# Scores and maxima of a two-layer transformer in two 64-row tiles of the TensorE array, with the causal mask of the first block of queries added by TensorE

## The reference, cut to what matters

```
x = x + L0_attn(ln(x)) + L0_ffn(ln(x))     # 32 query heads of 16 dims, 8 key heads; full softmax; GELU, 512 -> 2048 -> 512
x = x + L1_attn(ln(x)) + L1_ffn(ln(x))     # the same heads with rotary embedding, causal mask; SiLU gate, 512 -> 2*512 -> 512

scores = einsum('bqhd,bkhd->bhqk', q, k) * SM_SCALE
scores = where(mask, scores, finfo.min)    # second layer only: key <= query
probs  = softmax(scores)
ctx    = einsum('bhqk,bkhd->bqhd', probs, v)
```

## Time and profile before

| | |
|---|---|
| median of 3 runs | 596.59 us (593.41 to 599.78) |
| the profiled execution | 596.43 us |
| its span in the profile | 594.7 us |
| PE busy | 563.2 us, 95% |
| DVE busy | 456.5 us, 77% |
| ACT busy | 348.0 us, 59% |
| POOL busy | 232.6 us, 39% |

### The profile page before, as it was taken

How to read it: one execution, slowest core, us unless ns; L and a number is a source line. 1 busy time by engine, 2 the same in 40 slices (tenths; PEclk the granted TensorE clock), 3 DMA queues, 4 the chain that set the end, 5 groups by cost and what they waited for, 6 DMA issues and landing times.

```text
span 594.7 us, 10503 instructions
## 1 busy us (share of the span) xinstructions
PE 563.2 (95%) x3216; PEld 435.0 (73%) x3216; DVE 456.5 (77%) x1232; ACT 348.0 (59%) x598; POOL 232.6 (39%) x345
## 2 busy tenths in 40 slices
PE   3979999999999999999999999899899999998997
PEld 3967777777777878777787787667677778766754
DVE  6487987765666687577899678898998989789673
ACT  3667756664564676376677276357645564565451
POOL 6231334713304521313223115264745485364242
PEclk9999999999999999999999999999999999999999
DMA  6993452453223244315433323336443443434101
GB/s 200 130 317 103 120 142 69 113 157 107 79 82 108 80 124 136 90 40 174 126 128 99 113 78 101 90 107 143 134 117 89 104 130 109 125 108 133 29 6 68
DMA packets 30535, 67.02 MB, mean 113 GB/s; under 512 B 4880, under 2 KB 18192, under 8 KB 28560
## 3 DMA queue, kind: packets, MB, share of 16 engines
q1 hardware_dynamic: 21840, 38.04, 24.5%
q0 software_dynamic: 8640, 28.32, 15.9%
HBM read 50.87 MB, written 13.63 MB: 108 GB/s over the span
## 4 chain that ended last, share of the span: by engine, by line
PE 79%; DVE 8%; issue 5%; DMA 3%; POOL 2%; ACT 2%; DVEq 0%; POOLq 0%; ACTq 0%
PE banks L766 53%; PE banks L826 8%; PE banks L874 8%; PE banks L852 7%; DMA q_sb<-max_t 2%; DVE banks L1156 2%; PE banks L786 1%; PE banks L855 1%; POOL probs L708 1%; DVE neg_max L1156 1%; DVE o_tok L1177 1%; DVE x_res L1200 1%; PE banks L835 1%; DVE bn L1054 1%; DVE hid L1221 1%
## 5 line engine op out<-in xcount | busy, mean ns | idle before, releaser
L988 ACT ACTIVATE probs<-banks 128x512 f32<-128x512 f32 (+1 forms) x256 | 138.0, 545 | 187.5 <-PE banks L852 149.2
L766 PE MATMUL banks<-xnT,w_up 128*128 128x512 f32 x576 | 153.8, 400 | 0.2
L1161 DVE TENSOR_REDUCE neg_max<-banks 128x2 f32<-128x512 f32 x128 | 87.4, 688 | 79.3 <-PE banks L826 77.9
L766 PE MATMUL banks<-w_down,hid 128*128 128x512 f32 x480 | 127.4, 399 | 0.0
L766 PEld LDWEIGHTS banks<-xnT,w_up 128*128 128x128 f32 x576 | 102.1, 190 | 30.6 <-issue 12.9
L826 PEld LDWEIGHTS banks<-k_sb,q_sb 96*128 96x128 f32 x512 | 92.5, 191 | 23.6 <-issue 5.5
L1156 DVE CUSTOM_DVE_ANT_0 banks<-banks,mask_qk 128x128 f32<-128x128 f32 (+1 forms) x256 | 86.3, 375 | 25.5 <-PE banks L826 24.9
L826 PE MATMUL banks<-k_sb,q_sb 96*128 96x256 f32 (+1 forms) x512 | 100.0, 277 | 5.4 <-issue 3.2
L766 PEld LDWEIGHTS banks<-w_down,hid 128*128 128x128 f32 x480 | 85.2, 188 | 25.7 <-DVE max_t L1169 5.9
L708 POOL TENSOR_SCALAR_AFFINE_SELECT probs<-probs 128x256 f32<-128x256 f32 x128 | 59.5, 465 | 75.9 <-ACT probs L988 69.3
L852 PE MATMUL banks<-q_sb,k_sb 97*128 97x512 f32 x192 | 78.8, 410 | 8.4 <-DMA q_sb<-max_t 7.0
(11 more groups left out here) (79 smaller groups left out, 655.3 us busy)
## 6 DMA issues: line engine op xcount, KB each, us to landing
q_sb<-q_parts SPq DMA_DIRECT2D x60, 256.0 KB, 4.8
raw<-in_up POOLq DMA_DIRECT2D x48, 256.0 KB, 3.4
raw<-in_down POOLq DMA_DIRECT2D x40, 256.0 KB, 3.1
q_parts<-stage SPq DMA_DIRECT2D x30, 256.0 KB, 2.5
raw<-in_attn POOLq DMA_DIRECT2D x20, 256.0 KB, 3.6
k_parts<-stage SPq DMA_DIRECT2D x14, 256.0 KB, 2.5
k_sb<-k_parts SPq DMA_DIRECT2D x14, 256.0 KB, 4.1
out<-x_res SPq DMA_DIRECT2D x8, 256.0 KB, 2.1
```

The lines of the kernel that those rows point to most:

```text
L766: mm = nc.tensor.matmul(out_ap, lhs(a), rhs(b_), start=first and j == 0, stop=stop and j == 2, **kw)
L988: nc.scalar.activation(probs[:, i, 0:w], banks[:, ST_BANKS[k % 2], 0:w], ACT.Exp, scale=SCALES[n // B]).then_inc(exp_done, 1)
L1161: nc.vector.tensor_reduce(neg_max[:, s, 2 * g:2 * g + 2, t], banks[:, bank_of[x], :].rearrange("p (r t) -> p r t", r=2)[:, :, 0:w], AX.X, ...
```

## The change

- **Rows.** The low-by-low product is dropped from the scores: q is high, low, high and k high, high, low in 48 rows (`Q_PARTS`, `K_PARTS`), and the row for the maxima is the 49th. Two key heads then fit into the array's 128 rows, one at partition 0 and one at 64 (`HALF`), as two 64-row tiles. `q_sb` and `k_sb` are half as wide; zero rows and `fill` are gone.
- **Steps.** `m` and `st` now have 4 steps a unit (`STEPS`). A step issues for both tiles a = 0, 1 in turn: two `st` matmuls, into banks 0 and 1, and four `m` matmuls, into two work banks. The `st` pair waits until both exponentials of the step before are done.
- **Mask.** In the second layer, for the first block of queries, TensorE adds the mask to each of the two banks by a matmul of 16-bit operands (`identb`, `mask_qk`), in the whole array. VectorE then takes the maxima with a plain reduction, as in the first layer. For the second block nothing changes on VectorE.
- **Slots.** `st` and `m` stand in even slots. `pv` stands in slots 0 and 4 of the first layer (before: 1 and 5) and in slots 2 and 6 of the second, `norm` and `ctx` with it. The gates of the second layer (`gate`, `hidden`) are taken up behind the next `st` (`STEP`) instead of at once, what follows them one slot later. `COST` has 340 for `st` and for `m`.
- **Transfers.** SP issues 4 loads of q a unit (2 before), 2 of the maxima row (1), 2 of k (1), 4 stores of a first-layer pair (2), and for the first batch 6 and 12 transfers (4 and 8).

```diff
-ROWS = 96
-MROW = 96
+HALF = 64
+ROWS = 48
+MROW = 48
+STEPS = 4
+STEP = -1
...
-COST = {"up": 681, "down": 681, "wo": 693, "qkv": 363, "xn": 440, "v": 220, "st": 233, "m": 235, "mt": 110, "pv": 995}
+COST = {"up": 681, "down": 681, "wo": 693, "qkv": 363, "xn": 440, "v": 220, "st": 340, "m": 340, "mt": 110, "pv": 995}
...
-            return [(0, ("gate", c))]
-        return [(0, ("hidden", 1, c)), (2, ("hidden_hi", 1, c)), (3, ("hidden_lo", 1, c))]
+            return [(STEP, ("gate", c))]
+        return [(STEP, ("hidden", 1, c)), (3, ("hidden_hi", 1, c)), (4, ("hidden_lo", 1, c))]
...
+                if d == STEP:
+                    d = [k for k in range(1, 4) if g + k >= len(slots) or any(z[0] == "st" for z in slots[g + k])][0]
...
-        slots[1].append(("pv", u - 1, 1))
-        slots[2].append(("norm", u - 1, 0))
...
-    slots[5].append(("pv", u, 0))
+        slots[0 if u < LU else 2].append(("pv", u - 1, 1))
+        k = 1 if u < LU else 3
+        slots[k].append(("norm", u - 1, 0))
...
+    slots[4 if u < LU else 6].append(("pv", u, 0))
...
                     for r in range(2):
-                        mm = nc.tensor.matmul(banks[:, k, r * T:r * T + w],
-                                              q_sb[0:ROWS, u % RING, 2 * g + r, t * P:t * P + P], k_sb[0:ROWS, 4 * f + g, 0:w],
-                                              start=r == 0, stop=r == 1, skip_group_check=True)
+                        for a in range(2):
+                            rows = slice(HALF * a, HALF * a + ROWS)
+                            mm = nc.tensor.matmul(banks[:, ks[a], r * T:r * T + w],
+                                                  q_sb[rows, u % RING, 2 * c + r, t * P:t * P + P], k_sb[rows, 2 * f + c, 0:w],
+                                                  start=r == 0, stop=r == 1 and (n < B or t == 1), skip_group_check=True)
+                    if n >= B and t == 0:
...
+                        for a in range(2):
+                            first = banks[:, ks[a], :].rearrange("p (r t) -> p r t", r=2)[:, :, 0:P]
+                            mm = nc.tensor.matmul(first, identb[:, :], mask_qk[:, None, P:].to_broadcast([P, 2, P]),
+                                                  start=False, stop=True, skip_group_check=True)
                     mm.then_inc(wk_filled, 1)
...
-                    if k >= 2:
-                        pe.wait_ge(exp_done, k - 1)
...
+                    if st_index(u, j):
+                        pe.wait_ge(exp_done, 2 * st_index(u, j))
...
+                    for a in range(2):
+                        rows = slice(HALF * a, HALF * a + MROW + 1)
+                        mm = nc.tensor.matmul(banks[:, ST_BANKS[a], 0:2 * (T - q0)].rearrange("p (r t) -> p r t", r=2),
+                                              k_sb[rows, 2 * f + c, t * P:t * P + P],
+                                              q_sb[rows, u % RING, 2 * c:2 * c + 2, q0:], start=True, stop=True)
```

More of the change, by code:

```diff
@@ L159, in unit_slots @@
     b = n - B * L
[L160 removed]
+    slots = [[] for i in range(8)]
     for i in range(8):
[L162 to L165 removed]
+        j = i // 2
+        if i % 2 == 0:
+            slots[i].append(("st", u, j))
+        if i in (0, 2) and u + 1 < UNITS:
+            slots[i].append(("m", u + 1, j + 2))
+        if i in (4, 6) and u + 2 < UNITS:
+            slots[i].append(("m", u + 2, j - 2))
         if i == MT_SLOT and u + 1 < UNITS:
```

310 lines of the change are left out of this document (163 added, 147 removed).

## The result

The changed kernel takes 604.4 us (median of 4 executions, 601.9 to 605.1) against 595.0 us for the kernel before beside it (592.6 to 599.8). The ratio is 1.0137, with an interval from 1.0083 to 1.0191: slower by 1.4%. The profiled execution took 605.05 us with a span of 602.9.

What follows compares the result with a forecast made beforehand. TensorE was taken to bound the kernel, alone in the first layer. From the profiled 596.4 us, -9.9 + 5.0 + 2 - 8 = -10.9 gave 585.5 us; forecast 578 to 592, full range 570 to 604 us.

Steps and rivals of the forecast that it cites:

- First layer, TensorE, -9.9 us: First layer's score groups: row tiles gain .62 us a unit after mode-change costs, times 16, with nothing hiding it.
- Second layer, -3.0 us in sum (+5.0 and -8): Second layer's TensorE work +5.0 us, and fewer PE waits from 310 us on -8 us.
- -8: Half of PE's 16.4 us idle from 310 us on goes, mostly waits for late exponentials: -8 us.
- +5.0: Second layer's TensorE: wide groups gain .05 and .26, two narrow ones lose .31 each; +.31 a unit, times 16.
- rival E: Second layer: m waits for its second bank behind busy VectorE, one in three of 64 groups, 14.5 us: 608 us; chance .13.
- The start, +2 us: Start: six m groups replace twelve steps and four more transfers issue before the first q: +2 us (1 to 4).
- Nothing: the smaller loads of q and k lie beside other work: Smaller q and k loads, with zero fills and one memset less, lie beside other work: no time.
- VectorE 31 us less busy: Second layer's 64 narrow steps: VectorE's .89 us becomes about .4 each, 31 us less busy, moving nothing in PE's sum.
- Slower had .16: Chance of a result above 602.6 us: the two slower rivals, late second bank (.13) and row tiles not overlapping (.03).

Runs made afterwards that it cites:

- a_q_dve5: Changed kernel with q loads ahead of stores on SP, first-block mask back on VectorE, fourth example's statistics moved to unit 5: 587.4 us, ratio .9860.
- a_qfirst: Changed kernel with the q loads for the unit after next issued ahead of the stores in their slot on SP: 594.7 us, ratio .9943.
- b_split: Kernel before with the same bytes in twice as many SP transfers (stores, q, k, maxima each in two pieces): 605.2 us, ratio 1.0100.
- b_split8: Kernel before with twice as many SP transfers and each q load in eight pieces, 16 a unit: 674.0 us, ratio 1.1306.
- a_whole: Changed kernel with both matmuls of a pair in the whole array instead of row tiles, output not the reference's: 623.0 us, ratio 1.0402.

## Why the prediction was wrong, point by point

- **First layer, TensorE, -9.9 us: right.** Of the 96 rows of `m` before, 64 held parts of q or k and 32 zeros; 48 rows made room for two tiles, and their gaps and distances are those of the forecast within .02 us. From the first `st` to the second layer's, 3.8 us were added; less 9.7 us more of waits and three half-clock stretches (5.1), the streams gave -11.0. With the waits repaired, these 16 units took 317.1 us in a_q_dve5 (331.1 before): 14.0 less, of which 1.1 are fewer waits over .35 us and 1.7 the stretch at 42 us, which the profile of a_q_dve5 doesn't have. That leaves -11.2. Both ways 1 us of gain remains that the term doesn't have.
- **Second layer, -3.0 us in sum (+5.0 and -8): right in sum by luck, wrong in the term for waits.** From its first `st` to the end it took 5.9 us more, with five half-clock stretches (8.5): -2.6 at full clock. But PE is idle for 17.4 us from 310 us on, where it was 16.4, and the waits over .35 us are 16.0 us as before: of the -8 nothing came. The narrow group without `pv` costs about .84 us where the forecast had .91, which takes 2 us off the +5.0; the other 5 to 6 us of gain are in no term, and no run shows where they lie. The exponentials' waits went by more than half, as forecast, and three long ones for VectorE came, at 423, 483 and 538 us. That is rival E's engine, not its mechanism: few long waits for a masked maximum behind other work of VectorE (at 423 us behind .9 us of a split and 3.4 of the rotation, of which one L1162 took 1.96), not many for a second bank.
- **The start, +2 us: wrong sign.** The first `st` came 1.5 us earlier. The first `m` stands at 27.78 us, where 28.41 was and 30.5 allowed, although SP needs 8.75 us for twelve issues in place of 5.11: the smaller transfers landed sooner than the upper end had it, and the maxima row took 3.3 us from its issue at 36.86 us to `st` at 40.20, where it took 6.9 before (34.87 to 41.73). The one term that got a price for issues on SP was the one in which they didn't count.
- **"Nothing: the smaller loads of q and k lie beside other work": the step that failed.** Their bytes do, their number doesn't. .65 us an issue was in the earlier trace rows and was used for the start alone. Where a store of four meets loads of two and four, they hold SP for 5.7 us, and the q load stood last. The trace of before already had three waits of `m` for q, of .41 to .72 us, which the forecast didn't look for. So q had no slack, and the longer issue went straight into PE: the waits of `m` for q in the first layer grew from 1.7 to 7.2 us. a_qfirst and b_split show that from both sides. The other 4.0 us of the 9.7 are the wait for the bank of the maxima at 71 us, a second thing missed: when the order on VectorE shifts, a chain of short operations can fall beside GpSimd's splits. a_q_dve5 shows that this wait goes with the place of the chain.
- **No term for the clock: the larger miss.** A row of nines was read as a property of the kernel. It is one of an execution and its waits: behind the first `st` the longest of before's was 1.9 us. The forecast summed waits as if ten of .4 us and one of 4 cost the same. They don't: 8 stretches, 13.3 us by the mean clocks. Of the 19.5 us between forecast (-10.9) and result (+8.6, both against the profiled 596.4) the clock is 13.3 and the rest 6.2. That profile had the clock higher than most executions of the kernel before, though; by the medians (5.4 us lost before, 13.9 after) the clock's part is 8.5 us. Which waits cost the clock stays open.
- **VectorE 31 us less busy: 8.** The step multiplied mean durations of operations that overlap; "though the pairs overlap in part" hid a factor of four. It moved no time in the sum, but with the right figure the mask on TensorE would have been seen as a poor trade.
- **The chances.** Slower had .16, all of it in mechanisms that did not happen; the range ended at 604.0, and the result stands .4 us beyond it.

## What to carry to other kernels

Splitting a tile in two doubles the transfers. Count their issues on the queue that carries them, find what stands last there, and look in the trace of before for short waits on it: they say that there is no slack.

Where TensorE is the bound, weigh waits by their length, not their sum alone: a long one can cost another 1.7 us or more through the clock. Compare versions at equal clock as well as in time, since one kernel's own times differ by 2%, most of it through the clock.

Moving work by one slot is no safe small step. Put a short chain on VectorE where its result is needed and nothing waits behind it, rather than beside GpSimd's work.

## What the runs showed of the hardware that I had not expected

- VectorE operations on 128x2 elements take .16 us alone and up to 1.7 us when one falls beside a GpSimd `tensor_tensor` of 128x512 (1.2 us for L1110, 1.7 for L1113; 1.14 us for L1073 in the kernel before). They end .02 to .04 us after GpSimd's.
- In the changed kernel's profile each half-clock stretch began at the end of a wait or up to 1.9 us behind it, with the work back, and lasted 3.4 us; in other profiles some last 6.8 or 10.2 us, and some begin before the wait is over. All ten waits of 3.3 us and more in b_split8 behind its first `st` had one, that of 3.7 us in b_split had none.
- Two 64-row tiles, each with its own weights, start 3 to 4 ns apart and stream as one: the whole array in their place costs 16.6 us at full clock over 128 groups (a_whole). Entering and leaving the mode costs a gap of .09 us and an exposed weight load of .11 to .12 us, each way.
- The issue of one transfer on SP's queue takes .35 to .77 us for the sizes of these kernels; halving the bytes of a q load took it from .51 to .41 us.
